# VectorE's units split into single operations and put in a new order, in a fused gated-delta-rule and FFN kernel on one core

## The reference, cut to what matters

```python
x_act = jnp.tanh(x)                      # x: [8, 2048, 256]
static_out = jnp.einsum('bld,ed->ble', x_act, W)
# 16 heads of width 16; q = k = heads of x_act, v = heads of static_out
def step(S, inp):
    k_t, v_t, q_t = inp
    S = lam * S
    u = beta * (v_t - jnp.einsum('kv,k->v', S, k_t))
    S = S + k_t[:, None] * u[None, :]
    return (S, jnp.einsum('kv,k->v', S, q_t))
y = static_out + o_dyn
...                                      # y = layernorm(y) * ln_gamma + ln_beta
x = _layernorm(x + y)
gate = x @ wg.T; up = x @ wu.T           # int weights / 127, hidden 768
x = _layernorm(x + (silu(gate) * up) @ wd.T)
```

## Time and profile before

| | us |
|---|---|
| median of 3 runs (lowest, highest) | 1739.97 (1739.53, 1741.53) |
| the profiled execution's span | 1735.2 |
| TensorE busy | 1378.6 (79%) |
| VectorE busy | 1397.8 (81%) |
| ScalarE busy | 1103.3 (64%) |
| GpSimd busy | 803.9 (46%) |
| mean granted TensorE clock | 0.861 of full |

### The profile page before, as it was taken

How to read it: one execution, slowest core, us unless ns; L and a number is a source line. 1 busy time by engine, 2 the same in 40 slices (tenths; PEclk the granted TensorE clock), 3 DMA queues, 4 the chain that set the end, 5 groups by cost and what they waited for, 6 DMA issues and landing times.

```text
span 1735.2 us, 53678 instructions
## 1 busy us (share of the span) xinstructions
PE 1378.6 (79%) x21032; PEld 1073.9 (62%) x21032; DVE 1397.8 (81%) x3461; ACT 1103.3 (64%) x2357; POOL 803.9 (46%) x1106
## 2 busy tenths in 40 slices
PE   4357888888788888887898888888888787888765
PEld 3345666666666666666666666666666666666543
DVE  5578888888888888888888888888888887888752
ACT  3235666667667666766766666676667666666654
POOL 6023454444455454544555444454544445444543
PEclk9667889988888888888889888889988888888878
DMA  4546545545545555565555656545545654555210
GB/s 122 114 104 115 111 116 115 112 111 117 118 115 118 121 113 114 116 127 108 117 119 117 112 115 126 112 118 114 120 106 116 127 109 114 119 111 114 71 34 25
DMA packets 701325, 190.98 MB, mean 110 GB/s; under 512 B 620944, under 2 KB 688528, under 8 KB 701072
## 3 DMA queue, kind: packets, MB, share of 16 engines
q1 hardware_dynamic: 701072, 187.56, 50.7%
HBM read 103.55 MB, written 67.11 MB: 98 GB/s over the span
## 4 chain that ended last, share of the span: by engine, by line
PE 32%; DVE 23%; SPq 16%; DMA 11%; ACT 10%; issue 6%; POOL 1%; ACTq 0%; POOLq 0%; DVEq 0%
PE pc L185 12%; PE pu L256 4%; DMA scr_t<-t 4%; SPq L1121 4%; SPq L1112 4%; PE pf L219 4%; ACT v L758 4%; PE pg L256 3%; PE pf L230 3%; SPq L1155 3%; SPq L1168 3%; DMA scr_x<-xt 2%; DVE S L424 2%; DVE Sp L421 2%; PE pd L282 2%
## 5 line engine op out<-in xcount | busy, mean ns | idle before, releaser
L1017 POOL TENSOR_TENSOR hlo<-gate,hhi 128x512 f16<-128x512 f32 x192 | 228.9, 1195 | 310.6 <-ACT hhi L790 310.3
L185 PE MATMUL pc<-R,tb 128*128 128x32 f16 x4096 | 158.1, 188 | 125.6 <-DVE R L407 113.1
L185 PEld LDWEIGHTS pc<-R,tb 128*128 128x128 f16 x4096 | 147.8, 118 | 141.7 <-DVE R L407 125.7
L185 PE MATMUL pc<-S,e 128*128 128x32 f16 x4096 | 157.0, 186 | 74.5 <-DVE S L428 74.5
L185 PEld LDWEIGHTS pc<-S,e 128*128 128x128 f16 x4096 | 151.3, 117 | 91.7 <-DVE S L428 84.4
L282 PE MATMUL pd<-wd_t,hhi 128*128 128x256 f16 x768 | 174.4, 274 | 15.7 <-DVE xr L526 7.9
L185 PEld LDWEIGHTS pc<-U,kb 128*128 128x128 f16 x4096 | 154.6, 118 | 46.1 <-DVE U L415 44.0
L219 PEld LDWEIGHTS pf<-xb,e 128*128 128x128 f16 x4096 | 152.3, 118 | 47.5 <-DMA e<-scr_x 29.7
L185 PE MATMUL pc<-U,kb 128*128 128x32 f16 x4096 | 159.6, 190 | 22.3 <-DVE U L415 22.3
L219 PE MATMUL pf<-xb,e 128*128 128x32 f16 x4096 | 156.3, 192 | 23.7 <-DMA e<-scr_x 22.0
L282 PE MATMUL pd<-wd_t,hlo 128*128 128x256 f16 x768 | 174.0, 274 | 0.0
(11 more groups left out here) (134 smaller groups left out, 3282.9 us busy)
## 6 DMA issues: line engine op xcount, KB each, us to landing
xa<-L_attn_x SPq DMA_DIRECT2D x128, 128.0 KB
scr_x<-xt SPq DMA_DIRECT2D x64, 256.0 KB, 2.2
xb<-scr_x SPq DMA_DIRECT2D x256, 64.0 KB, 2.9
e<-scr_x SPq DMA_DIRECT2D x256, 64.0 KB, 3.6
scr_g<-gs SPq DMA_DIRECT2D x32, 512.0 KB, 3.5
gh<-scr_g SPq DMA_DIRECT2D x32, 512.0 KB, 3.5
kb<-k SPq DMA_DIRECT2D x512, 32.0 KB, 2.2
scr_t<-t SPq DMA_DIRECT2D x64, 256.0 KB, 4.4
```

The lines of the kernel that those rows point to most:

```text
L185: last = pe.matmul(pc2[:, :, cols], stationary(h, a), moving[:, :, cols], start=a == 0, stop=a == 1)
L1017: pool.tensor_tensor(hlo[:, t, :], gate[:, t % 2, :], hhi[:, t, :], ALU.subtract).then_inc(SEM["hl"], 1)
```

## The change

Three things are changed. No instruction is added or removed, and no tile, shape or semaphore wait of an operation differs.

1. VectorE's helpers are split into single operations: `dve_rest` into high, sum and low, `dve_update` into high and low, `dve_state` into high, sum and low, `dve_key_norms` into square sums and key norms, and each column of `dve_invert` into scale and add.
2. `dve_step` calls them in a new order, written in the diff.
3. The boundary between two steps is put elsewhere in every list, and the tails are gone: the steps run from -3 to NS+2 (34), and `live` and `later` leave out what doesn't exist. On TensorE, ScalarE, GpSimd and SyncE the order of the calls stays the same up to the last chunks; the calls of chunks 30 and 31 come in the order of a whole step. On ScalarE that puts `act_variance(30, 3, ...)` and `act_last_norm(30, ...)` ahead of `act_variance(31, 2, ...)` and `act_first_norm(31, ...)`. On GpSimd `pool_attention_norm(31)` comes behind `pool_multiply(30, 5)`, and `pool_mean` and `pool_bias(30, 3)` ahead of `pool_mean` and `pool_bias(31, 2)`. On TensorE chunk 31's FFN begins up 0, gate 0, gate 1, gate 2, up 1, up 2 in place of gate 0, up 0, gate 1, up 1, gate 2, gate 3. SyncE's order is the same throughout.

The diff, cut. Lines of `dve_step` that are removed are those of the kernel above; its new lines stand in full.

```diff
 
-        FIRST, LAST = -1, NS
+        FIRST, LAST = -3, NS + 3
...
 
+        def later(q):
+            return 1 <= q < NS
+
...
         def pe_step(pe, s, p):
-            if live(s - 2):
-                pe_up(pe, s - 2, p, 0)
-                pe_gate(pe, s - 2, p, 0)
-                pe_gate(pe, s - 2, p, 1)
-                pe_gate(pe, s - 2, p, 2)
-                pe_up(pe, s - 2, p, 1)
...
             if live(s):
                 pe_keys_by_update(pe, s, p, 3)
-
-
-
-        def dve_rest(dve, q, p, w):
+            if live(s - 1):
+                pe_up(pe, s - 1, 1 - p, 0)
+                pe_gate(pe, s - 1, 1 - p, 0)
+                pe_gate(pe, s - 1, 1 - p, 1)
+                pe_gate(pe, s - 1, 1 - p, 2)
+                pe_up(pe, s - 1, 1 - p, 1)
+
+
+        def dve_rest_high(dve, q, p, w):
             dve.wait_ge(SEM["kp"], n_of("kp", q, w + 1))
             if w % 2 == 0:
                 dve.wait_ge(SEM["v"], n_of("v", q, w // 2 + 1))
...
             dve.scalar_tensor_tensor(R[:, :], pc[:, 0:D], dcol[:, 0:1], v[:, p, w, :],
                                      ALU.mult, ALU.add).then_inc(SEM["r1"], 1)
+
+        def dve_rest_sum(dve, q, p, w):
             dve.wait_ge(SEM["r1"], n_of("r1", q, w + 1))
             dve.scalar_tensor_tensor(Sp[:, :], pc[:, D:2 * D], dcol[:, 0:1], R[:, :],
                                      ALU.mult, ALU.add).then_inc(SEM["r0"], 1)
+
+        def dve_rest_low(dve, q, p, w):
             dve.wait_ge(SEM["r0"], n_of("r0", q, w + 1))
             dve.wait_ge(SEM["rh"], n_of("rh", q, w + 1))
             dve.scalar_tensor_tensor(R16[:, 1, :], Sp[:, :], RS, R16[:, 0, :], ALU.mult, ALU.subtract)\
                .then_inc(SEM["r"], 1)
 
-        def dve_update(dve, q, p, w):
+        def dve_update_high(dve, q, p, w):
             dve.wait_ge(SEM["uh"], n_of("uh", q, w + 1))
             dve.scalar_tensor_tensor(R[:, :], pc[:, 0:D], 1.0 / TS, U16[:, w % 2, 0, :], ALU.mult, ALU.subtract)\
                .then_inc(SEM["u0"], 1)
+
+        def dve_update_low(dve, q, p, w):
             dve.wait_ge(SEM["u0"], n_of("u0", q, w + 1))
             dve.scalar_tensor_tensor(U16[:, w % 2, 1, :], pc[:, D:2 * D], 1.0 / TS, R[:, :], ALU.mult, ALU.add)\
                .then_inc(SEM["u"], 1)
 
-        def dve_state(dve, q, p, w):
+        def dve_state_high(dve, q, p, w):
             dve.wait_ge(SEM["sp"], n_of("sp", q, w + 1))
             dve.wait_ge(SEM["sl"], n_of("sl", q, w + 1))
             dve.scalar_tensor_tensor(Sp[:, :], pc[:, 0:D], sc[:, BETAS:BETAS + 1], S[:, :],
                                      ALU.mult, ALU.add).then_inc(SEM["s1"], 1)
+
+        def dve_state_sum(dve, q, p, w):
             dve.wait_ge(SEM["s1"], n_of("s1", q, w + 1))
             dve.scalar_tensor_tensor(S[:, :], pc[:, D:2 * D], sc[:, BETAS:BETAS + 1], Sp[:, :],
                                      ALU.mult, ALU.add).then_inc(SEM["s0"], 1)
+
+        def dve_state_low(dve, q, p, w):
             dve.wait_ge(SEM["s0"], n_of("s0", q, w + 1))
             dve.wait_ge(SEM["sh"], n_of("sh", q, w + 1))
             dve.scalar_tensor_tensor(S16[:, 1, :], S[:, :], SS, S16[:, 0, :], ALU.mult, ALU.subtract)\
...
 
-        def dve_key_norms(dve, q, p):
+        def dve_square_sums(dve, q, p):
             dve.wait_ge(SEM["y1"], n_of("y1", q - 2))
             dve.wait_ge(SEM["sq"], n_of("sq", q))
             dve.tensor_reduce(nb[:, p, :, :], xa[:, :, :].rearrange("p n (h k) -> p n h k", h=H),
                               AX.X, ALU.add).then_inc(SEM["nr"], 1)
+
+        def dve_key_norms(dve, q, p):
             dve.wait_ge(SEM["nr"], n_of("nr", q))
             dve.tensor_scalar(nb[:, p, :, :], nb[:, p, :, :], sc[:, BETAR:BETAR + 1], -0.5 / RS,
                               ALU.mult, ALU.add).then_inc(SEM["nb"], 1)
...
-        def dve_invert(dve, q, p, cols):
-            for j in cols:
-                m, i = slice(0, j), slice(j + 1, C)
-                if j == 1:
-                    dve.wait_ge(SEM["tc"], n_of("tc", q))
-                else:
-                    dve.wait_ge(SEM["tf"], n_of("tf", q, 2 * j - 1))
-                dve.tensor_tensor(tmp[:, m, 0:C - 1 - j, :],
-                                  tt[:, m, j:j + 1, :].to_broadcast([P, j, C - 1 - j, NW]),
-                                  gh[:, i, j, :][:, None].to_broadcast([P, j, C - 1 - j, NW]), ALU.mult)\
-                   .then_inc(SEM["tf"], 1)
-                dve.wait_ge(SEM["tf"], n_of("tf", q, 2 * j))
-                dve.tensor_tensor(tt[:, m, i, :], tt[:, m, i, :], tmp[:, m, 0:C - 1 - j, :], ALU.add)\
-                   .then_inc(SEM["tf"], 1)
+        def dve_invert_scale(dve, q, p, j):
+            m, i = slice(0, j), slice(j + 1, C)
+            if j == 1:
+                dve.wait_ge(SEM["tc"], n_of("tc", q))
+            else:
+                dve.wait_ge(SEM["tf"], n_of("tf", q, 2 * j - 1))
+            dve.tensor_tensor(tmp[:, m, 0:C - 1 - j, :],
+                              tt[:, m, j:j + 1, :].to_broadcast([P, j, C - 1 - j, NW]),
+                              gh[:, i, j, :][:, None].to_broadcast([P, j, C - 1 - j, NW]), ALU.mult)\
+               .then_inc(SEM["tf"], 1)
+
+        def dve_invert_add(dve, q, p, j):
+            m, i = slice(0, j), slice(j + 1, C)
+            dve.wait_ge(SEM["tf"], n_of("tf", q, 2 * j))
+            dve.tensor_tensor(tt[:, m, i, :], tt[:, m, i, :], tmp[:, m, 0:C - 1 - j, :], ALU.add)\
+               .then_inc(SEM["tf"], 1)
 
...
         def dve_step(dve, s, p):
+            if live(s - 1):
+                dve_statistics(dve, s - 1, 1 - p, 1)
                 dve_statistics(dve, s - 1, 1 - p, 2)
+            if live(s):
+                dve_store_inverse(dve, s, p, 1)
+            if live(s - 2):
+                dve_multiply(dve, s - 2, p, 1)
             if live(s - 1):
                 dve_statistics(dve, s - 1, 1 - p, 3)
             if live(s):
+                dve_rest_high(dve, s, p, 0)
+                dve_rest_sum(dve, s, p, 0)
+            if live(s - 1):
+                dve_moments(dve, s - 1, 1 - p)
+            if live(s - 2):
+                dve_multiply(dve, s - 2, p, 2)
+            if live(s + 1):
+                dve_gram(dve, s + 1, 1 - p, 0)
+            if live(s - 2):
+                dve_multiply(dve, s - 2, p, 3)
+                dve_multiply(dve, s - 2, p, 4)
+            if live(s + 1):
+                dve_gram(dve, s + 1, 1 - p, 1)
+            if live(s):
+                dve_rest_low(dve, s, p, 0)
+            if live(s - 2):
+                dve_multiply(dve, s - 2, p, 5)
             if live(s + 1):
                 dve_scale_keys(dve, s + 1, 1 - p, 0)
+                dve_gram(dve, s + 1, 1 - p, 2)
             if live(s - 1):
                 dve_load_residual(dve, s - 1, 1 - p)
+            if live(s):
+                dve_update_high(dve, s, p, 0)
+                dve_update_low(dve, s, p, 0)
             if live(s - 2):
                 dve_add_ffn(dve, s - 2, p, 0)
                 dve_add_ffn(dve, s - 2, p, 1)
+            if live(s + 1):
+                dve_gram(dve, s + 1, 1 - p, 3)
+            if live(s):
+                dve_state_high(dve, s, p, 0)
+                dve_state_sum(dve, s, p, 0)
             if live(s - 1):
                 dve_attention_norm(dve, s - 1, 1 - p, 0)
+            if live(s):
+                dve_state_low(dve, s, p, 0)
+            if live(s - 1):
                 dve_attention_norm(dve, s - 1, 1 - p, 1)
                 dve_attention_norm(dve, s - 1, 1 - p, 2)
             if live(s + 1):
                 dve_scale_keys(dve, s + 1, 1 - p, 1)
             if live(s - 2):
                 dve_add_ffn(dve, s - 2, p, 2)
                 dve_add_ffn(dve, s - 2, p, 3)
             if live(s):
+                dve_rest_high(dve, s, p, 1)
+            if live(s - 1):
+                dve_attention_norm(dve, s - 1, 1 - p, 3)
+            if live(s):
+                dve_rest_sum(dve, s, p, 1)
+                dve_rest_low(dve, s, p, 1)
+            if live(s + 1):
+                dve_square_sums(dve, s + 1, 1 - p)
+            if live(s):
+                dve_update_high(dve, s, p, 1)
+                dve_update_low(dve, s, p, 1)
+                dve_state_high(dve, s, p, 1)
+                dve_state_sum(dve, s, p, 1)
+                dve_state_low(dve, s, p, 1)
+            if live(s + 1):
+                dve_mask_gram(dve, s + 1, 1 - p)
+            if live(s):
+                dve_rest_high(dve, s, p, 2)
+                dve_rest_sum(dve, s, p, 2)
+                dve_rest_low(dve, s, p, 2)
+            if live(s + 1):
+                dve_invert_scale(dve, s + 1, 1 - p, 1)
+                dve_invert_add(dve, s + 1, 1 - p, 1)
+                dve_invert_scale(dve, s + 1, 1 - p, 2)
+                dve_invert_add(dve, s + 1, 1 - p, 2)
+            if live(s):
+                dve_update_high(dve, s, p, 2)
+                dve_update_low(dve, s, p, 2)
+            if live(s + 1):
```

(91 more changed lines are left out.)

279 lines of the change are left out of this document (28 added, 251 removed).

## The result

The changed kernel takes 1777.3 us (median of 4 runs, 1773.0 to 1783.8) against 1740.8 for the kernel before beside it (4 runs): ratio 1.0203, 95% interval 1.0172 to 1.0234. It is slower, as forecast, but by 36.6 us where 17 were forecast, and outside the range. The profiled execution has a span of 1775.9, 40.7 more than before.

The account below looks back on a forecast made before the run. No engine's sum bounds it: the recurrence's serial round holds windows 1 to 3, TensorE the FFN half. 1735.2 + 4.6 (steps) + 12.1 (end) = 1751.9, plus 4.8 to the median gives 1757 us; range 1742 to 1773.

Parts of the forecast that it names:

- Window 3's correction, the loss: VectorE, window 3: two inverse operations ahead make the correction 0.50 late; x1lo's extra addition 0.10; TensorE's FFN starts 0.60 late.
- How lateness meets the clock: TensorE's FFN half: the 0.60 is taken back at full clock, but goes through where the stretch begins at half clock.
- rival (c): TensorE idles longer ahead of each FFN, so most full-clock steps become half-clock ones: 1778 us; chance 0.11.
- The first multiplication, the gain: VectorE's first gate multiplication comes 1.0 earlier, ending TensorE's wait at the third up tile: half a microsecond to be won.
- Window 0: VectorE's reordered window 0: update 0 is 0.3 late, back to +0.09 by window 1; bounds 0 to 0.4 a step.
- Transfers: SyncE's queue still sets the inverse's store; in steps waiting on transfers lateness is hidden, the change doing -0.1 to +0.1.
- Rival (b): The inverse's earlier store moves the transfer chain; some 13 steps gain 0.75: -10 us, 1747; chance 0.12.
- The split: VectorE's helpers split: adds nothing; a dependent pair pulled apart saves about 0.12, 1.6 us of VectorE's time a step.
- (a): VectorE is the bound, its 1.6 us a step lying wholly on the path: 1718 us; chance 0.09.
- (e): VectorE pairs pulled apart save nothing, so 0.24 a step is not earned: +7.4, 1764 us; chance 0.02.
- The end: From chunk 30's last down products to chunk 31's FFN 16.6 instead of 2.4; chunk 30's FFN -2.1; in all +12.1.
- The term for chunk 31's FFN: Last chunk: its FFN loses the last norms from its middle but begins at the lower clock after long idle: 0.

Follow-up runs that it names:

- a2: Kernel after with the add of column 4 back ahead of state 2 and the scale of column 5 back behind window 3's rest: 1770.4 us, ratio 1.0156.
- b6: Kernel before with only the add of column 4, scale of column 5 and add of column 9 placed as the change places them: 1771.6 us, ratio 1.0158.
- a4: Kernel after, order untouched, with GpSimd's three attention-output operations over 1 of 16 heads in windows 2 and 3: 1753.2 us, ratio 1.0058.
- f3: Kernel after with five unused TensorE products added in window 3: 1768.5 us, ratio 1.0149.
- c1: Kernel after with the add of column 4, scale of column 5 and add of column 9 put back, and the old end: 1740.3 us, ratio 0.9997.
- t1: Kernel before with four of the eight transfers spreading each chunk's packed keys left out from the second chunk on: 1711.4 us, ratio 0.9838.
- u1: Kernel before, whole, with four of the eight key-spreading transfers issued by ScalarE instead of SyncE: 1725.5 us, ratio 0.9923.
- c2: c1 with five unused TensorE products added in window 3: 1741.6 us, ratio 1.0002.
- a1: Kernel after with ScalarE's variances and last norm of chunk 30, and GpSimd's bias, back behind chunk 31's transposed x1: 1775.8 us, ratio 1.0186.
- f2: a2 with five unused TensorE products added in window 3: 1751.7 us, ratio 1.0064.
- f1: Kernel before with five unused TensorE products added in window 3: 1738.6 us, ratio 0.9999.

## Why the forecast was right in sign and wrong in size

Of the 24.0 us by which the profiled execution missed the forecast (40.7 against 16.7), 19.0 lie in the steps, 4.7 in the end and the rest in the start. The step that failed is the price of window 3's correction and of x1lo: 0.60 for the moved operations, at the lengths that they had alone. Beside GpSimd they made the FFN 1.8 late, and the term that multiplied this, half-clock steps counted from the old trace and held fixed, came out at 12 of 23.

**The rule that the runs leave.** A step takes the longer of two: about 50.7 by the transfers, or the offset and what follows it, which in the kernel after is as little as 24.7 at full clock and 26.2 to 26.7 in most half-clock steps. Kernel before: 24.0 + 26.7 is 50.7, so by this even a half-clock step would be hidden, an estimate, as it has none (in its full-clock steps it is never under 25.8). Kernel after: 25.8 + 24.7 = 50.5 in a full-clock step, no loss at all; 25.8 + 26.2 = 52.0 in a half-clock step. a2: 24.5 + 26.7 = 51.2, every step. b6: 25.5 + 26.7 = 52.2. The medians in the traces are 50.5, 52.1, 51.2 and 52.3. (That a full-clock step can lie below 50.7 because the transfers catch up in the longer one ahead of it is my reading; no run shows it.)

By the prediction's own parts:

- *Window 3's correction, the loss.* The place was right, and so was the order's own cost (a4: 0.6); this is the step that failed. I took the moved operations' lengths from the earlier trace rows, where they stood alone, and got 0.50 and 0.10. Beside GpSimd they take 0.4 and 0.5 more; the correction came 1.2 late and the FFN 1.8, not 0.60.
- *How lateness meets the clock.* I had it that a late FFN counts in half-clock steps alone, and that held (f3). But I counted 5 such steps of 24 from the old trace and held the number fixed. The change itself made 12 to 15 of 23. It was rival (c) that said so: 1778 against 1777.3. Its condition came true, though its sum had 0.6 and 0.6 a step where the trace has 1.4 to 1.5 in half-clock steps and none in the others; at a chance of 0.11 it was priced too low. That its total is so near is luck: its end is 4.8 us too small and its steps 2.2 too large.
- *The first multiplication, the gain.* No wait for the gate is left ahead of up 2, as said. In the kernel after nothing came of it: the wait vanishes in b6 too, where the multiplication was not moved. That a later FFN gives VectorE the time for it is the likely reason.
- *Window 0.* VectorE's idle time ahead of update 0 fell from a mean of 1.04 (steps 4 to 27) to 0.01, not by 0.3. It cost nothing that can be measured: c1 keeps the order (0.33).
- *Transfers.* The inverse's store no longer stands right behind the residual's load in most steps: it is 0.12 behind it in 11 of 32 chunks (26 before), and in the rows below 1.7. The waits for kb fell from 22.6 to 7.8 us. I read the waits for transfers as cover in some steps; on the mean of all steps they were the limit itself, as t1 and u1 show. Rival (b) was thus right that the transfers' chain bounds the kernel and wrong on what the change does to it: where the FFN isn't late (c1, c2) SyncE stays the holder, as the forecast had it. SyncE's queue after, step 13:

```profile
779.32 2.66 SPq L1081 DMA_DIRECT2D res<-L_attn_x  x4
783.70 1.77 SPq L1046 DMA_DIRECT2D scr_t<-t  x2
```

- *The split, and rivals (a) and (e).* VectorE's list isn't what sets 50.7: t1 and u1 are shorter with it untouched. It may be part of the floor below. Whether a pair pulled apart saves its 0.12 on the path none of these runs shows, as both limits lie elsewhere; (e)'s sum, which took it away, can't be told from the forecast's by them.
- *The end.* The chain was forecast at 16.6 and is 16.3. The FFN of chunk 30 gained 1.2, not 2.1. The term for chunk 31's FFN, which "begins at the lower clock after a long idle: 0", is the one that failed here: it is +4.2. And the chain had a second lock, chunk 31's residual behind chunk 30's sums (a1), without which undoing the first was worth 5.6.

Left open: why nearly all steps of a2 take over 5.8 us for the first twenty products at an offset of 24.5 and none of a4 at 24.6 (12 of them 4.8 to 5.8). TensorE waits 0.67 ahead of the FFN in the one and 0.40 in the other; no run varies that alone.

## What to carry to other kernels

Before an operation is moved, look at what the other engines run at its new place and not only at its length where it stands; here what it met there cost 24 us. Look too for an operation that takes twice as long as its twin of the same shape: the trace of before had one in every step. Where TensorE's clock can change, an idle time that a change adds can cost twice, and the share of half-clock steps in the old trace is no forecast of the new. When several unlike repairs all stop near one number, as here at 50.7 to 51.0 us, look for the other limit: here the queue that issues the transfers, four of which another engine had time for.

## What the runs showed of the hardware

In the kernel after, a VectorE tensor_tensor of the inverse, with both operands in SBUF, that starts while one of GpSimd's three tensor_tensor runs ends 0.17 to 0.25 us after that one: 0.36 becomes 0.72 (mean of invert_scale(5), 26 steps), 0.38 becomes 0.88 (invert_add(9)); with short GpSimd operations both are back at 0.37. The wait lies inside VectorE's row, and no idle time is shown ahead of it. Operations with one operand in PSUM don't do this: in the kernel before, the rest's and the state's first operations take 0.482 beside one of GpSimd's three (mean of 92) and 0.480 without (of 164). The Trainium skill has this rule: SBUF — State Buffer, "SBUF: two separate sides", says that a VectorE operation with two SBUF inputs and a GpSimd operation that reads SBUF lock the same pair of ports for a whole instruction, so that the later one blocks. The trace agrees (0.36 became 0.72), and it was to be read there before the forecast.

Five products of 512 columns a step that nobody uses made one kernel 18.7 us faster (f2, from a2) and left another as it was (f1).
